# A graph block on one core: where the second norm is applied, and where attention, its exponential and its copies stand in the order

## The reference, cut to what matters

```python
h = jnp.maximum(_layernorm(x), 0.0)
x = x + attention(h, W, adj)          # 4 heads of 32, masked by adj, softmax over all 128 tokens
h = jnp.maximum(_layernorm(x), 0.0)   # the second norm
h1 = relu(adj @ (h @ Wg0 + bg0))      # two graph layers
h2 = relu(adj @ (h1 @ Wg1 + bg1))
for p in 1, 2, 3, 4:                  # windows of p tokens; an LSTM over each window
    last = lstm_last(Wih[p-1], Whh[p-1], ..., windows of p tokens of h2)
    h2[:, every p-th token] = last
x = x + h2
```

## Time and profile before

| | |
|---|---|
| median of 3 runs | 523.53 us (523.16 to 525.69) |
| the profiled execution, its own time | 523.03 us |
| its span in the profile | 521.2 us (1.8 us lie around it) |
| mean granted clock of TensorE | 0.988 |
| busy: PE, DVE, ACT, POOL | 91%, 82%, 67%, 43% of the span |
| start of the iterations on DVE (first row maxima) | k=3 at 50.70, k=4 at 68.37, k=14 at 232.02, k=16 at 264.21 us |

### The profile page before, as it was taken

How to read it: one execution, slowest core, us unless ns; L and a number is a source line. 1 busy time by engine, 2 the same in 40 slices (tenths; PEclk the granted TensorE clock), 3 DMA queues, 4 the chain that set the end, 5 groups by cost and what they waited for, 6 DMA issues and landing times.

```text
span 521.2 us, 10204 instructions
## 1 busy us (share of the span) xinstructions
PE 475.5 (91%) x3528; PEld 395.1 (76%) x3528; DVE 427.9 (82%) x929; ACT 350.4 (67%) x577; POOL 223.2 (43%) x229
## 2 busy tenths in 40 slices
PE   3767999999999999999979999999999999999994
PEld 2546878777777778777767777889999987888784
DVE  3958779889998899998985788888888889976775
ACT  2455777778777787777766777777766665665551
POOL 1476667776777667775442021221121222222211
PEclk9998999999999999999997999999999999999999
DMA  7323100000000000000000000000000000000225
GB/s 209 105 82 94 30 1 2 1 0 0 0 0 0 0 0 1 0 0 1 2 1 1 1 0 1 1 0 2 0 1 3 0 0 1 0 1 1 82 82 161
DMA packets 18779, 11.29 MB, mean 22 GB/s; under 512 B 662, under 2 KB 17724, under 8 KB 18748
## 3 DMA queue, kind: packets, MB, share of 16 engines
q1 hardware_dynamic: 17052, 10.03, 6.8%
q10 hardware_dynamic: 1696, 0.87, 0.6%
HBM read 6.70 MB, written 4.19 MB: 21 GB/s over the span
## 4 chain that ended last, share of the span: by engine, by line
PE 45%; DVE 32%; issue 10%; ACT 7%; POOL 2%; DMA 2%; DVEq 1%; SPq 0%; ACTq 0%; POOLq 0%
PE ps L934 25%; DVE rmax L1170 6%; PE ps L787 4%; PE ps L883 3%; DVE arena L1172 3%; DVE S_hi L1253 3%; PE ps L888 2%; DVE arena L1240 2%; DVE X L1193 2%; PE ps L839 2%; DVE stats L1097 2%; PE ps L776 2%; DMA X<-in_x_dram 2%; ACT arena L616 2%; ACT arena L608 2%
## 5 line engine op out<-in xcount | busy, mean ns | idle before, releaser
L630 ACT ACTIVATE arena<-ps,bias 128x512 f32<-128x512 f32 (+1 forms) x207 | 121.1, 624 | 47.0 <-PE ps L934 46.1
L594 ACT ACTIVATE arena<-ps 128x512 f32<-128x512 f32 (+1 forms) x128 | 89.9, 702 | 53.8 <-PE ps L787 28.8
L574 POOL TENSOR_TENSOR arena<-arena 128x512 f32<-128x512 f32 (+1 forms) x36 | 43.4, 1205 | 178.0 <-ACT arena L630 178.0
L934 PE MATMUL ps<-H_hi,W_hi 128*128 128x512 f32 (+2 forms) x207 | 75.6, 365 | 2.8 <-DVE S_lo L1255 2.0
L934 PE MATMUL ps<-H_lo,W_hi 128*128 128x512 f32 (+2 forms) x207 | 75.0, 362 | 0.0
L934 PE MATMUL ps<-H_hi,W_lo 128*128 128x512 f32 (+2 forms) x207 | 75.0, 362 | 0.0
L776 PE MATMUL ps<-ident,arena 128*128 128x128 f32 x448 | 60.7, 279 | 13.3 <-ACT arena L599 8.1
L776 PEld LDWEIGHTS ps<-ident,arena 128*128 128x128 f32 x448 | 52.1, 152 | 20.5 <-ACT arena L599 9.8
L537 POOL TENSOR_TENSOR arena<-arena 128x512 f32<-128x512 f32 x32 | 41.4, 1293 | 56.5 <-ACT arena L599 38.0
L519 POOL TENSOR_TENSOR rstd<-veps,minus_half 128x4 f32<-128x4 f32 x32 | 43.0, 1345 | 44.5 <-DVE veps L1105 44.5
L1240 DVE TENSOR_TENSOR arena<-arena 128x512 f32<-128x512 f32 (+1 forms) x53 | 34.0, 641 | 23.9 <-ACT arena L616 23.8
(11 more groups left out here) (107 smaller groups left out, 1001.2 us busy)
## 6 DMA issues: line engine op xcount, KB each, us to landing
X<-in_x_dram SPq DMA_DIRECT2D x16, 256.0 KB, 2.8
out_dram<-X SPq DMA_DIRECT2D x14, 256.0 KB, 2.4
out_dram<-X ACTq DMA_DIRECT2D x2, 256.0 KB, 3.9
arena<-in_L_gnn_W_dram ACTq DMA_DIRECT2D x1, 128.0 KB, 3.2
wg<-in_L_gnn_Wg_dram ACTq DMA_DIRECT2D x2, 64.0 KB, 2.3
bg_rows<-in_L_gnn_bg_dram SPq DMA_DIRECT2D x6, 0.5 KB
wv<-in_L_gnn_W_dram ACTq DMA_DIRECT2D x1, 64.0 KB, 3.2
adj_sb<-in_adj_dram SPq DMA_DIRECT2D x1, 64.0 KB, 3.4
```

Of the source, the lines that this page charges most:

```text
L574: g_.tensor_tensor(ig[:, it.buf, 0:w], sig_i[:, it.buf, 0:w], tanh_g[:, it.buf, 0:w], ALU.mult)\
L594: a_.activation(to, psum, func).then_inc(ready, 1)
L630: a_.activation(to[:, it.buf, 0:w], ps[:, 4 * it.par + j, 0:w], func, bias=bias[:, col:col + 1])\
L934: l = mm(o, wt, v, start=m == 0, stop=m == len(terms) - 1)
```

## The change

The second norm loses its DVE step and the relu on ACT. DVE makes one small tensor, `shift_2` = -mean * rstd for the four batches (128x4), and ACT makes relu(x * rstd + shift_2) in four activations of 128 columns, straight from X, with scale and bias as operands of each partition. POOL's second `add_halves` no longer waits for DVE. On ACT the second exponential and the two copies of the transposed probabilities come ahead of the copies of k and v; the second norm stands ahead of `read_hT` (it was behind), `read_att` ahead of `u1T`, the last LSTM gate ahead of `u2T`. On PE `put_mask` of the first two heads goes ahead of gate 0, `attend` from behind `graph_linear_1` to right behind the scores, `attended` to right behind `graph_linear_1`, and gate 2 ahead of the last `graph_mix`. On DVE `output_lo` goes ahead of `first_h_part`.

```diff
@@ tiles and semaphores
+        shift_2 = sb("shift_2", [P, GB])
-        xn2 = tokens_first()
-        hn2 = xn2.rearrange("p b d -> p (b d)")
+        hn2 = take(GT)
@@ POOL
-                    if s.back:
-                        pool.wait_ge(xn2_ready, s.k - 1)
                     add_halves(s, 1)
@@ ACT
+            def second_norm(g):
+                act.wait_ge(shift2_ready, g + 1)
+                for b in range(GB):
+                    l = a_.activation(hn2[:, b * D:(b + 1) * D],
+                                      X[:, ds(g * GB + b, 1), :].rearrange("p a d -> p (a d)"), ACT.Relu,
+                                      bias=shift_2[:, b:b + 1], scale=rstd[:, 1, b:b + 1])
+                l.then_inc(hn2_ready, 1)
@@ ACT, last iteration: read(hn2, hn2, xn2_ready, ...) becomes second_norm(k - 2)
@@ ACT, iteration
-                if s.front:
-                    read(kT[:], psQ, k_done, k + 1, k_ready)
-                    read_v(s)
                 if s.mid:
                     exp(s, 1)
                     read_probT(s, 0)
                     read_probT(s, 1)
+                if s.front:
+                    read(kT[:], psQ, k_done, k + 1, k_ready)
+                    read_v(s)
+                second_norm(k - 2)
                 if s.next1:
                     read_hT(psX[s.back], k + 2, 1 - s.par)
-                read(hn2, hn2, xn2_ready, k - 1, hn2_ready, ACT.Relu)
                 if s.finish:
                     ...
                     first_gate(k - 3, 0, act_i, 0, 0.5)
+                if s.mid:
+                    read_att(s)
                 read(u1T[:], psA, u1_done, k - 1, u1T_ready)
...
-                if s.mid:
-                    read_att(s)
-                read(u2T[:], psA, u2_done, k - 1, u2T_ready)
                 if s.finish:
                     ...
                     first_gate(k - 3, 2, act_o, 3, 0.5)
+                read(u2T[:], psA, u2_done, k - 1, u2T_ready)
@@ PE
                     transpose_prob(s, 1)
-                first_gate(s, 0, 0)
                 if s.front:
                     pe.wait_ge(probT_ready, k * 2 - 1)
                     put_mask((0, 1))
+                first_gate(s, 0, 0)
+                if s.front:
                     pe.wait_ge(probT_ready, k * 2)
                     put_mask((2, 3))
                     pe.wait_ge(k_ready, k + 1)
                     scores()
+                attend(s)
                 pe.wait_ge(hn2_ready, k - 1)
...
                 graph_linear_1().then_inc(z1_done, 1)
-                attend(s)
-                pe.wait_ge(h1_ready, k - 1)
-                interleave([], graph_mix(h1, u2_done, by_token_batch_first(psA)))
-                first_gate(s, 2, 3)
                 if s.next1:
                     pe.wait_ge(hT_hi_ready, k + 2)
                 attended(s)
+                first_gate(s, 2, 3)
+                pe.wait_ge(h1_ready, k - 1)
+                interleave([], graph_mix(h1, u2_done, by_token_batch_first(psA)))
@@ DVE
+            def second_shift(g):
+                dve.wait_ge(rstd2, g + 1)
+                v_.scalar_tensor_tensor(shift_2[:], mv[:, 1, :, 0], -1.0, rstd[:, 1, :], ALU.mult, ALU.mult)\
+                    .then_inc(shift2_ready, 1)
@@ DVE, iteration and last iteration: normalize(1, k - 2, ...) becomes second_shift(k - 2), and
+                if s.finish:
+                    output_lo(k - 3)
                 if s.after:
                     first_h_part(k - 4)
-                if s.finish:
-                    output_lo(k - 3)
```

More of the change, by code:

```diff
@@ L376, in gnn_block @@
         x2_ready = sem("x2_ready")
-        xn2_ready = sem("xn2_ready")
+        shift2_ready = sem("shift2_ready")
         hn2_ready = sem("hn2_ready")
@@ L1320, in last_iteration @@
                 add_attention(k)
-                normalize(1, k - 2, xn2, rstd2, xn2_ready)
+                second_shift(k - 2)
                 output_lo(k - 3)
```

## The result

The changed kernel takes 528.50 us in the median of 6 runs (527.54 to 529.51), the kernel before 523.35 us (522.56 to 525.69, 6 runs). The ratio is 1.0085, with a 95% interval of 1.0062 to 1.0108: slower by 0.85% (4.4 us), and by 5.15 us between the two medians. The forecast was 523.0 us with 519.5 to 528.0. Two of the six executions of experiment 8 were in a slower state (590.60 and 922.77 us) and are left out of its median.

The account below looks back on a forecast made before the run. Order was taken to bound the kernel, by a chain over DVE, PE and ACT, with DVE and PE nearly full. +1.4 - 1.0 - 0.5 - 0.3 = -0.4 on 523.0 us gave 522.6, by run median 523.1, stated 523.0; range 519.5 to 528.

Parts of the forecast that it names:

- the steady iterations: Loop iterations: +0.57 us on PE against -0.53 before it, so nothing within 0.1 us; DVE's saved 0.9 us worth 0.
- The second norm's price n: Four 128-column activations on ACT: 0.33 us each, n = 1.33 us, free up to about 1.45 us.
- rival 3: ACT's chain to gate 1 binds, from n = 1.45: 528 us at n = 1.8, 532 at 2.16; chance 0.16.
- The chain over PE: `H_ready` to gate 1 on PE: `attend` +1.01 us, masks -0.44, against `output_lo` -0.53 before it; nothing within 0.1 us.
- Rival 2: DVE's work bounds after all, and the 0.9 us that leave it shorten each iteration: 514 us; chance 0.06.
- The addition to X: DVE's addition in the loop collides less with POOL's `add_halves`: 0.2 us each second iteration, 1.0 us gained.
- The first iterations: Start, iterations 2 and 3: more ACT work ahead of `read_hT` makes gate 1 late, +1.4 us, bounds 0 and 2.2.
- Iteration 15: No `read_hT`, so earlier `output_lo` and the shorter addition show in part: -0.5 us, bounds 0 and -1.0.
- The last iterations: Iteration 16 about -0.6 us, iteration 17 +0.3; together -0.3, bounds +0.5 and -2.5.
- rival 1: Iteration 16's clock holds at the upper level as PE's idle stretch shrinks, saving 2 us: 521.0 us; chance 0.18.
- rival 4: POOL's first norm beside DVE's `first_cell_part` slows it by 0.4 us in 10 iterations: 527 us; chance 0.12.
- the forecast's own range: Total time from the bounds of the forecast's terms: 520.5 to 526 us.

Follow-up runs that it names:

- experiment 8: experiment 3 with only the read of gate 0 moved ahead of `read_hT` on ACT; 519.13 us against 524.55, ratio 0.9898.
- experiment 1: The changed kernel with POOL's second `add_halves` again waiting, for `shift2_ready`; 523.88 us against 524.25, ratio 1.000.
- experiment 2: The kernel before with only POOL's wait for the normalized tile taken out; 536.98 us against 524.25, ratio 1.0240.
- experiment 3: The changed kernel's order with the second norm as before (`normalize` on DVE, one relu on ACT, POOL's wait); 520.76 us against 524.25, ratio 0.9918.
- experiment 4: The kernel before, order kept, with `second_shift`, four activations at the relu's place, POOL waiting for the shift; 528.41 us against 524.25, ratio 1.0070.
- experiment 6: experiment 3 with attention and its read moved behind gate 1, gate 0 read ahead of `read_hT`; 510.52 us against 523.45, ratio 0.9743.
- experiment 9: The changed kernel with only attention and its read on ACT moved behind gate 1; 534.60 us against 524.55, ratio 1.0184.

## Why the prediction was wrong

**The step that failed** stands under the steady iterations: "POOL's second `add_halves` starts about 1.2 us earlier; the row sums that need it are read behind `first_cell_part`, so that is 0 too". I asked who waits for the result and not what the earlier start would run beside. It came 1.7 to 1.9 us earlier after S and runs beside `second_shift`, from the same release, and that takes 1.24 us instead of 0.15. With it fell "the new wait for `shift2_ready` ends near S+9.8": it ended at S+10.35 (164.71), after ACT was there, and ACT started 0.47 us late (by 163.89 + 0.49), with `read_hT` and gate 0 behind it. Experiment 1 gives 0.48 us an iteration back by that wait alone, 4.8 of the loop's +5.0 us, and experiment 2 shows the same collision in the kernel before.

**The second norm's price n** was mis-sized: 1.33 taken, 1.55 measured (480 ns each, 386 to 390 ns apart). The Trainium skill, ScalarE: Activation LUTs, What ACT_TABLE_LOAD costs, which the prediction cited beside it, gives 1.54, and the trace agrees. In my sum the operands were too cheap: a 512-column copy of 0.60 us less 0.32 for the columns is 0.28, so the two operands cost 0.20 us and not 0.16 (an estimate from these rows). The free part of n was 1.45, and rather less, since gate 1 in the earlier trace rows starts at S+13.17 and not at 13.24; so this term alone made gate 1 wait for ACT. With the collision away the four activations put gate 1 at S+13.27, against S+13.10 with one relu (experiments 1 and 3), and cost 1.9 us in the loop. The mechanism of rival 3, ACT's chain to gate 1, was thus the one that came, with 0.16 of the chance; it had two causes and I had priced one.

**The chain over PE** was read rightly. Gate 0 starts at S+8.81 where 9.38 stood in the short kind (forecast: some 0.5 us nearer) and at S+8.73 where 9.60 stood in the long one. Attention costs what its row says (165.53 to 166.55, 1.02 us). With one relu on ACT (experiment 3) gate 1 starts at S+13.17 in the short kind, where it stood before, so the earlier `H_ready` and masks did pay for attention; in the long kind it comes 0.28 us nearer, which is what the addition to X got shorter. That the removed 0.9 us of DVE only lengthens DVE's wait is right as well: it stood 0.41 to 0.45 us before L1200 and stands 1.6 us before it now, in experiment 1 too, where the iterations are as long as before. Rival 2 never had room.

**The addition to X** lasts 0.69 in the loop's median (0.92 before), as forecast, and 0.69 instead of 0.97 in the long kind, where the collision was; order alone shows the gain, -1.6 in the loop against the -1.0 taken.

**The first iterations** cost 1.6 us, 1.4 were taken; by experiments 3 and 4 either part alone brings a loss of that size (+1.0 and +1.8), so the two don't add. Iteration 15 gave 0.4 (0.5 taken).

**The last iterations:** rival 1 came true in the profiled execution, the clock held. Iteration 16 and the next under the windows' view, of before and then of the changed kernel:

```profile
264.00:286.00 22.00, 17.52 (x140) 14.27 (x132) 15.45 (x35) 14.20 (x23) 7.08 (x7) 0.84 0.00 1
```
```profile
270.00:292.00 22.00, 15.98 (x126) 12.85 (x125) 16.21 (x42) 16.47 (x27) 7.72 (x8) 1.00 0.00 1
```

PE idled for 1.34 us before gate 0 and then 1.49 us for hn2, and the granted clock stayed at the upper level, 2.4 GHz, where a single 2.21 us gap had been followed by the lower one, 1.2 GHz. The stretch to the end is 1.8 us shorter; I had taken 0.3 and put 2 us on the rival. But the shorter gap is not shown to be the reason. Gate 0 of iteration 16 in the changed kernel, and then in experiment 1 with the windows' row behind it:

```profile
279.14 0.50 PE L847 MATMUL ps<-H_hi,W_hi 128*128 128x512 f32 x1 [1.34 <-DVE H_lo L1234]
```
```profile
274.50 0.80 PE L849 MATMUL ps<-H_hi,W_hi 128*128 128x512 f32 x1 [1.36 <-DVE H_lo L1236]
```
```profile
274.00:280.00 6.00, 5.50 (x44) 4.29 (x45) 3.15 (x5) 3.02 (x7) 3.88 (x4) 0.50 0.00 0
```

There the same gap went with the lower level. And of the changed kernel's six runs three have a mean granted clock of 0.993 or 0.994 and take 527.5 to 527.9 us, the other three 0.990 and 529.1 to 529.5; where the clock fell in those no trace shows.

**POOL's first norm beside `first_cell_part`** (rival 4) cost little in the changed kernel: L1215 has a median of 693 ns and a maximum of 785. In experiment 4 it was 0.85 us. The Trainium skill, SBUF — State Buffer, SBUF: two separate sides, speaks of an exclusive lock on the pair that the two engines share, held for the whole instruction. For `second_shift` beside L537 the trace agrees: DVE's operation ends 0.03 us after POOL's. For `first_cell_part` beside L527, whose instructions last 0.79 us, it agrees less: the operation was held up by 0.16 us in experiment 4, and by nothing in the long kind and 0.03 us in the short kind of the changed kernel, though it started in the middle of such an instruction.

**The range.** The low end of the forecast's own range, 520.5, is not the sum of the lower bounds as given, which is 6.0 us below 523.5 and so 517.5. It played no part in the miss, which was on the other side.

## What to carry to other kernels

Before a wait is taken out because nobody needs its order, look at what the released instruction will run beside, on DVE and POOL above all: a 0.15 us operation on the way to a third engine can become as long as POOL's whole instruction. Work taken off an engine that waits anyway gives nothing, and the engine it goes to may hold the next link of the chain: count the receiving engine's instructions one by one up to the step that the chain needs, as here up to gate 0's read. And the first place for a long step that nobody waits for is behind the link, not before it: attention behind gate 1 was worth 8 to 9 us (experiments 8 and 6) where the whole change cost 5. It is worth this only where the link waits in PE's own order; where it waited for ACT the same move gained nothing and cost 6 us (experiment 9). Last, a kernel whose iterations come in two kinds is compared kind by kind: the means hid that experiment 9 loses in the loop in one kind only, by an addition on DVE and half sums on POOL that had moved together.

## What of the hardware was not expected

A DVE operation with two SBUF operands of 128x4 elements lasted 1237 ns in the median beside POOL's 128x512 addition and 154 ns in the median without it. Four DVE instructions of 128 columns, 1.12 us together, took 2.90 us beside three of POOL's additions, in the kernel before without its wait. A 128x512 addition on DVE ended 0.55 us behind POOL's 128x256 addition whenever that one was late enough to hold it up, for 0.83 to 1.08 us instead of 0.69 by POOL's start.

POOL's power on 128x4 elements (L519) has a median of 1.43 us in the kernel before and of 1.03 in the changed one, for the same work. It goes by the order on DVE: the median is 1.38 to 1.43 in the three kernels with the old order (before, 2 and 4) and 1.03 in the eight with the new one. In the old order the power that gives `rstd2` starts beside `first_h_part`, with two operands in SBUF, in the new one beside `output_lo`, with one in PSUM. Whether this is the reason no run shows.
